# Third block's rounded parts kept in tiles that live on, and the first retention heads' rows loaded and padded one stage earlier

## The reference

```python
x = x + softmax_attention(layernorm(x))     # rope, RMS norm of q and k, 16 heads of 8, causal
x = x + spline_ffn(layernorm(x))
x = x + retention(layernorm(x))             # below
x = x + spline_ffn(layernorm(x))
x = x + linear_attention(layernorm(x))
x = x + conv_moe(layernorm(x))              # MoE block 1: causal attention with rope, then experts
x = x + rwkv(layernorm(x))
x = x + conv_moe(layernorm(x))              # MoE block 2, the same weights

def retention(x):
    q, k = split(x @ W_qk + b_qk); v = x @ W_v + b_v          # 16 heads, q and k 8 wide, v 16 wide
    scores = einsum('bhtd,bhsd->bhts', q, k) * mask            # decay by gamma per head, causal
    denom = clip(abs(scores).sum(-1, keepdims=True), 1.0, 50000.0)
    ret = einsum('bhts,bhsv->bthv', scores / denom, v)
    ret = ret * rsqrt(mean(ret * ret, -1) + EPS)
    return ((x @ W_g + b_g) * ret) @ W_o + b_o
```

## Time and profile before

| | |
|---|---|
| runs, us | 2375.11, 2379.26, 2385.63 |
| profiled execution, its own time | 2386.77 us |
| its span in the trace | 2385.0 us (so 1.77 us lie outside the span) |
| TensorE, mean granted clock | 0.877 of full speed |
| TensorE busy | 1936.0 us, 81% |
| VectorE, ScalarE, GpSimd busy | 1677.1 (70%), 1374.0 (58%), 455.2 us (19%) |
| attention stages begin at | 66.95, 1114.80 and 1803.78 us |
| chunk stage of the retention, then its heads stage | 619.8 to 644.4 us, from 644.6 us |

### The profile page before, as it was taken

The page is one execution under the profiler, slowest core; times in us unless marked ns, Lnnn a source line. Parts: engine busy times, 40 slices in busy tenths (PEclk is TensorE's granted clock), DMA queues, the critical chain, the costliest instruction groups (busy, mean ns, idle before and its releaser), DMA issues. The chain is left out here.

```text
span 2385.0 us, 38939 instructions
## 1 busy us (share of the span) xinstructions
PE 1936.0 (81%) x12970; PEld 1046.3 (44%) x12970; DVE 1677.1 (70%) x4201; ACT 1374.0 (58%) x2027; POOL 455.2 (19%) x816
## 2 busy tenths in 40 slices
PE   5899899975699974687899899957557999999839
PEld 3433333333477753464333333337334333333338
DVE  6688798747466777567798898632696897888423
ACT  4257667865378865435367677832543466677712
POOL 4010120110245430220101110133000010211233
PEclk8599999996899986897699999978865799999959
DMA  7342020001201000006032020014024402200034
GB/s 218 81 72 37 3 38 2 2 33 32 79 38 40 38 18 1 1 1 174 17 59 38 3 38 2 2 47 176 25 59 118 72 13 26 38 2 2 2 106 159
DMA packets 47527, 113.89 MB, mean 48 GB/s; under 512 B 11952, under 2 KB 21426, under 8 KB 43144
## 3 DMA queue, kind: packets, MB, share of 16 engines
q1 hardware_dynamic: 40308, 96.84, 17.2%
q0 software_dynamic: 5088, 11.24, 1.5%
q10 hardware_dynamic: 1964, 3.70, 0.4%
HBM read 62.39 MB, written 32.64 MB: 40 GB/s over the span
## 5 line engine op out<-in xcount | busy, mean ns | idle before, releaser
L1124 ACT ACTIVATE probs<-score 128x1024 f32<-128x1024 f32 x960 | 822.8, 897 | 429.1 <-PE score L1223 423.1
L1294 DVE TENSOR_REDUCE max_part<-stat 128x1 f32<-128x512 f32 x1152 | 724.7, 682 | 94.0 <-PE stat L1175 86.2
L1237 PE MATMUL pv<-probs,v_ones 128*9 128x512 f32 (+3 forms) x3840 | 458.4, 551 | 0.6 <-ACT out_turned L1117 0.6
L1291 DVE CUSTOM_DVE_ANT_0 masked_scores<-stat,mask_row 128x128 f32<-128x128 f32 (+3 forms) x768 | 346.8, 487 | 145.3 <-PE stat L1175 142.2
L1175 PE MATMUL stat<-first_group_k,first_group_q 64*128 64x512 f32 (+2 forms) x960 | 364.2, 496 | 41.5 <-PEq L708 16.1
L1175 PE MATMUL stat<-group_k,group_q 64*128 64x512 f32 (+2 forms) x960 | 337.4, 407 | 16.2 <-DVE max_part L1294 7.7
L1175 PEld LDWEIGHTS stat<-first_group_k,first_group_q 64*128 64x128 f32 x960 | 176.7, 215 | 288.3 <-DVE max_part L1294 174.6
L1175 PEld LDWEIGHTS stat<-group_k,group_q 64*128 64x128 f32 x960 | 157.8, 185 | 279.2 <-DVE max_part L1294 162.1
L1223 PE MATMUL score<-first_group_q,first_group_k 64*128 64x512 f32 x960 | 251.3, 423 | 32.0 <-ACT probs L1124 19.6
L1223 PE MATMUL score<-group_q,group_k 64*128 64x512 f32 x960 | 229.8, 418 | 40.4 <-ACT probs L1124 31.3
L1920 ACT ACTIVATE abs_act_ps<-abs_act_ps 128x1024 f32<-128x1024 f32 (+3 forms) x176 | 167.5, 952 | 46.8 <-PE abs_act_ps L1873 43.2
(11 more groups left out here) (369 smaller groups left out, 2488.7 us busy)
## 6 DMA issues: line engine op xcount, KB each, us to landing
tile_wv<-expert_wv SPq DMA_DIRECT2D x38, 512.0 KB, 3.2
q_parts<-early_parts_t SPq DMA_DIRECT2D x21, 512.0 KB, 3.8
k_parts<-early_parts_t SPq DMA_DIRECT2D x12, 512.0 KB, 4.7
group_k<-k_parts SPq DMA_DIRECT2D x24, 256.0 KB, 11.9
group_q<-q_parts SPq DMA_DIRECT2D x24, 256.0 KB, 18.2
head_q<-q_parts SPq DMA_DIRECT2D x32, 128.0 KB
head_k<-k_parts SPq DMA_DIRECT2D x32, 128.0 KB
first_group_q<-pad_rows SPq DMA_DIRECT2D x6, 512.0 KB, 5.6
```

The lines of the kernel that those rows point to most:

```text
L1124: nc.scalar.activation(probs[:, n % PSLOTS, :, 0:width], sc[m % 2][:, :, 0:width], ACT.Exp, scale=scale).then_inc(slot_read.sem, 1)
L1237: last = nc.tensor.matmul(acc[32 * h:32 * h + D + 1, f:BANK], v9[:, kt, g * HG + h, :], probs[:, (2 * t + h // 2) % PSLOTS, h % 2, 0:BANK ...
L1291: nc.vector.tensor_tensor_reduce(masked[:, at % 2, 0:width], ring[n % RBANKS][:, 0:width], w["mask_row"][:, BANK - width:BANK], 1.0, NEG, ...
L1294: nc.vector.reduce_max(into, ring[n % RBANKS][:], AX.X).then_inc(stat_used.sem, 1)
```

## The change

Three edits go together.

1. The parts of block 2 (the third) are no longer written to `early_parts_t` but to a tile that lives on: `group_q` of the attention, which is now allocated ahead of the qkv stage, or in the retention one slot of `head_q`. Then SyncE's wait for the stores of block 2 is taken out of the qkv stage; the next stage waits for it, where it waited for all stores already.
2. In the retention SyncE loads the rows of heads 0 and 1 in `chunk_stage`, behind its wait for the stores, and GpSimd clears the unused partitions there too, at the end of its own work: four memsets of 4096 columns, for queries and keys. VectorE clears none any more.
3. SyncE's loop over the other 14 heads is written out.

```diff
@@ qkv_stage
-        early = k.sb("early_parts_t", [P, NQ - 1, 2, PARTS, BANK], F32, ctx)
-        parts = [early[:, c] for c in range(NQ - 1)] + [turned_sb]
+        late = len(turned_sb)
+        early = k.sb("early_parts_t", [P, NQ - late, 2, PARTS, BANK], F32, ctx)
+        parts = [early[:, c] for c in range(NQ - late)] + turned_sb
...
-                for c in range(NQ - 1):
+                for c in range(NQ - late):
                     sp.wait_ge(stored[c].sem, stored[c].at(NS))
@@ attention_stage
-        uq, uk = ([first_rows[n], k.sb(f"group_{what}", [P, PAIRS, T], F32, ctx)] for n, what in enumerate("qk"))
+        uq, uk = [first_rows[0], first_rows[2]], [first_rows[1], k.sb("group_k", [P, PAIRS, T], F32, ctx)]
@@ chunk_stage, SyncE
                     wait_parts(sp, parts_stored(k))
+                    for h in range(2):
+                        ahead.load(sp, h, h)
@@ chunk_stage, GpSimd, behind its loop
+                if ahead:
+                    wait_parts(pool, parts_stored(k))
+                    pool.wait_ge(staged.sem, staged.at(NS * NT))
+                    ahead.pad(pool)
@@ new
+class RetentionRows:
+    def load(self, sp, h, par):
+        for a in range(PARTS):
+            at = slice(a * PARTS * D, (a + 1) * PARTS * D)
+            sp.dma_start(self.q[at, par, :], bcast(self.q_dram[h, a], 0, PARTS)).then_inc(self.loaded[par].sem, 16)
+            sp.dma_start(self.k[at, par, :], self.k_dram[h]).then_inc(self.loaded[par].sem, 16)
+    def pad(self, pool):
+        n = 0
+        for tile in (self.q, self.k):
+            for unused in (slice(KROWS, 2 * KROWS), slice(2 * KROWS, P)):
+                n += 1
+                self.nc.gpsimd.memset(tile[unused].rearrange("r b t -> r (b t)"), 0.0).then_inc(self.padded.sem, 1)
+                pool.wait_ge(self.padded.sem, self.padded.at(n))
@@ retention_heads_stage
-                wait_parts(sp, stored)
-                body(0, 0, first=True)
-                body(1, 1, first=True)
-                with sp.Fori(1, H // 2) as n:
-                    for par in range(2):
-                        body(2 * n + par, par)
+                for h in range(2, H):
+                    body(h, h % 2)
...
-                for par in range(2):
-                    for n, rows in enumerate(PADDED):
-                        nc.gpsimd.memset(km[rows, par, :], 0.0).then_inc(k_padded.sem, 1)
-                        pool.wait_ge(k_padded.sem, k_padded.at(2 * par + n + 1))
...
-                for par in range(2):
-                    for rows in PADDED:
-                        nc.vector.memset(qm[rows, par, :], 0.0).then_inc(q_padded.sem, 1)
@@ turned_parts
+    last = k.sb("parts_t", [P, 2, PARTS, BANK], F32, ctx)
+    if spare is None:
+        return [last[:]]
+    return [spare[:, 0].rearrange("p (n a t) -> p n a t", n=2, a=PARTS), last[:]]
```

More of the change, by code:

```diff
@@ L1472, in spline_ffn_stage, with chunk_stage @@
         stats.done()
-def chunk_stage(k, w, kk, v, q_t, k_t, width, keep, out, inner=True):
+def chunk_stage(k, w, kk, v, q_t, k_t, width, keep, out, inner=True, ahead=None):
     nc = k.nc
@@ L1724, in done, with __init__, retention_heads_stage @@
         self.scaled.done(NQ)
-def retention_heads_stage(k, w, v, parts_dram, part, diag, ret, gate, x):
+class RetentionRows:
+    COUNT = 2 * PARTS * 16
+    def __init__(self, k, parts_dram, ctx):
+        self.nc = k.nc
+        self.q, self.k = (k.sb(f"head_{n}", [P, 2, T], F32, ctx) for n in "qk")
+        self.loaded = [k.counter(f"ret_rows_loaded{n}") for n in range(2)]
+        self.padded = k.counter("ret_rows_padded")
+        self.q_dram = parts_dram[0][:, :, 0, :].rearrange("a (h d) t -> h a d t", d=D)
+        self.k_dram = parts_dram[1].rearrange("(h d) a t -> h a d t", d=D)
+    def load(self, sp, h, par):
[10 more added lines that the diff above has]
+                pool.wait_ge(self.padded.sem, self.padded.at(n))
+    def done(self):
+        for sig in self.loaded:
+            sig.done(self.COUNT * H // 2)
+        self.padded.done(4)
+def retention_heads_stage(k, w, v, rows, part, diag, ret, gate, x):
     nc = k.nc
@@ L1758, in retention_heads_stage @@
         o_ps = k.ps("own_out_ps", [P, BANK], ctx)
-        loaded = [k.counter(f"ret_rows_loaded{n}") for n in range(2)]
         a_full, a_used, d_full, d_used = (k.counter("abs_" + n) for n in ("act_full", "act_used", "dve_full", "dve_used"))
@@ L1965, in _ @@
                 take_out(H - 1)
-        for par in range(2):
-            loaded[par].done(NL * H // 2)
+        rows.done()
         cleared.done(5)
-        q_padded.done(4)
-        k_padded.done(4)
         a_full.done(NA * H)
@@ L2465, in first_group_rows, with turned_parts @@
 def first_group_rows(k, ctx):
[L2466 to L2471 removed]
+    return [k.sb(f"{name}", [P, PAIRS, T], F32, ctx) for name in ("first_group_q", "first_group_k", "group_q")]
+def turned_parts(k, ctx, spare=None):
+    last = k.sb("parts_t", [P, 2, PARTS, BANK], F32, ctx)
+    if spare is None:
+        return [last[:]]
+    return [spare[:, 0].rearrange("p (n a t) -> p n a t", n=2, a=PARTS), last[:]]
 def softmax_layer(k, w, qkv, wo, parts_dram, rows, parts_t, x, turns=(), first_norm=None):
     y = qkv[:, :, 0:C]
[L2477 removed]
+    attention_stage(k, w, qkv, parts_dram, rows, parts_t[-1], float(D) ** -0.5, y, first_norm)
     output_stage(k, w, [(y, wo)], x, turns)
@@ L2504, in retention_layer @@
                 transpose_stage(k, [(qkv[:, :, 0:C], q_t)], w["ident"])
-                chunk_stage(k, w, qkv[:, :, C:2 * C], qkv[:, :, 2 * C:], q_t, None, VD, w["bd16"][:], ret, inner=False)
-        retention_heads_stage(k, w, qkv[:, :, 2 * C:], parts_dram, part, diag, ret, gate, x)
+                chunk_stage(k, w, qkv[:, :, C:2 * C], qkv[:, :, 2 * C:], q_t, None, VD, w["bd16"][:], ret, inner=False, ahead=rows)
+        retention_heads_stage(k, w, qkv[:, :, 2 * C:], rows, part, diag, ret, gate, x)
         output_stage(k, w, [(gate[:, :, b * C:(b + 1) * C], w["w_o_r"][:, b, :]) for b in range(2)], x,
```

37 lines of the change are left out of this document (12 added, 25 removed).

## The result

The changed kernel took 2374.94 us (median of 19 runs, 2365.51 to 2383.22), the kernel before 2380.80 us beside it (19 runs, 2375.11 to 2391.14). The ratio is 0.9965, 95% interval 0.9953 to 0.9977: faster by 8.3 us, or 5.5 to 11.2 (the ratio is that of the means, 2373.77 and 2382.06 us; the medians lie 5.9 us apart). Forecast were -9.9 us and 2369.4 us. The sign and the main places were right; two terms of the sum were too small, with opposite signs, so that the total came out nearer than its parts.

A forecast was written before the change was run, and what follows sets the result against it. No engine bounds the whole, so stage seams were read. Terms -4.6 - 4.5 + 0.6 - 0.2 - 1.2 gave -9.9 us, 2369.4 us (chance 0.62); terms' range -7.5 to -11.8, 8-in-10 range 2361 to 2379 us.

The forecast's parts named there:

- The waits that go: End of the qkv stage in MoE blocks 1 and 2: SyncE's store wait disappears, -4.6 and -4.5 us.
- What is late next: Start of both MoE attentions: block 1's row loads contend with stores still running, 0 to 0.8 us a block, +0.6 together.
- Shifted by 4.6 us, the last load is issued at 1115.3 and lands at 1117.2: MoE block 1's attention start: row loads keep their issue pace and landing delay, only 4.6 us earlier.
- rival C: MoE attention starts: SyncE held up issuing, loads as late as before; about -2 us left, 2377 us; chance 0.10.
- Retention, end of its qkv stage: SyncE's store wait there ends barely later than ScalarE's store: -0.2 us, bounds 0 and -0.6.
- Heads: Retention's chunk-to-heads seam: DMA wait gone, GpSimd's clears end the chunk stage; -1.2 us, range -0.4 to -2.1.
- it waits for TensorE each time: Retention heads: SyncE's written-out loop changes nothing, 0 us.
- First block: End of its qkv stage: VectorE's last cast hides SyncE's wait, so 0 us.
- its terms' own range: Whole sum with contention, heads and retention terms at their ends: -7.5 to -11.8 us.
- rival D: Retention's chunk stage: GpSimd's memsets at twice the price, ending at 669, about +3 us; chance 0.02.
- A: MoE attentions: TensorE's clock stays up after the shorter gap; -18 us in all, 2361 us; chance 0.15.
- B: MoE attentions: clock falls into block 2's pattern, 8.2 us each; with two blocks 2385.8 us; chance 0.11.

The follow-up runs named there:

- e4: Changed kernel with the third block's three stores issued in the softmax layers' attention, behind the loads of block 1's rows; 2371.96 us, ratio 0.9946.
- e13: Changed kernel with clears behind the norm, third block's stores behind block 1's loads, ScalarE's last-block stores behind its copy of v; 2359.01 us, ratio 0.9893.
- e1: Kernel before with the first edit and the written-out loop; retention heads' rows loaded and cleared in the heads stage as before; 2376.48 us, ratio 0.9974.
- e2: Changed kernel with SyncE's wait for the third block's stores put back, so only the early rows and clears and the written-out loop; 2383.44 us, ratio 1.0003.
- e11: Changed kernel with three quarters of GpSimd's clears moved into the retention's qkv stage, behind VectorE's first-block decay; 2364.51 us, ratio 0.9905.
- e3: Changed kernel with ScalarE's two stores of the last block started behind its copy of v; one execution, 2374.34 us.

## Why the prediction was right, point by point

*The waits that go* (-4.6 and -4.5): the attention begins 4.5 and 4.4 us earlier, counted from VectorE's last cast. From SyncE's last store to the attention's start it was 0.65 us, not 0.5. Right.

*What is late next* (+0.6 for both, bounds 0 to 1.6): 1.24 and 0.87 us are lost by the copy-out, 2.1 together, and 1.03 and 1.01 by the turn. This is one of the two mis-sized terms, and it lies outside its bounds. The step that failed is "Shifted by 4.6 us, the last load is issued at 1115.3 and lands at 1117.2". The load was not issued as before and then late by its bytes; the issue itself slowed, so that the last load is issued 7.05 us behind the attention's beginning instead of 5.09. e4 shows that the third block's stores in front, SyncE's own, are the cause: with them out of the way it is 5.0 again (3.6 and 4.4 in e13, where ScalarE's stores are out of the way too). It is the mechanism of rival C at a quarter of its price. The other part of the step, that 0.8 us of delay are free because the turn waits for GpSimd anyway, was right in kind and put a little low: rows 2.0 us late, turn 1.0 us late in both blocks, so 1.0 us was free. The first copy-out is late by what the turn is, within the 0.6 us by which two traces of the same code differ there.

*Retention, end of its qkv stage* (-0.2): 0.03 us, from the spline addition to the chunk stage. ScalarE's store was the last already.

*Heads* (-1.2): from the chunk stage's last copy to TensorE's first matmul 12.78 us before, 11.19 after: -1.6. The memsets took 14.2 us as worked out; they ended at 652.5 instead of 655.0 because the whole stage lies 2.5 us earlier, most of it from the first block; and TensorE began 0.5 us behind them. One reading of the rows was incomplete, without harm: only 3.5 of the 5.1 us lay behind all memsets before, since VectorE's last one ended at 653.6.

Behind TensorE's first matmul another 1.9 us came. This is the other mis-sized term: the sum ends at that matmul and puts what comes after it at nothing, so that the heads gained 3.4 us in all (2.3 without head 14, below), outside the bounds of 0.4 to 2.1. The first head takes 0.5 us less: the granted clock, 0.50 at first in both, rises to 1.00 some 7 us into it instead of 9 (over the first 10 us 0.63 instead of 0.53). At head 3 (counted from 0) TensorE waited 0.37 us for its rows before and 0.16 after, which gives 0.2 us; the other traces have from 0.1 to 0.5 there. And 1.05 us lie at head 14, where it waited before and not after:

```profile
847.81 0.66 PE L1883 MATMUL abs_dve_ps<-head_q,head_k 128*128 128x128 f32 x4 [0.90 <-DMA head_k<-k_parts]
```

That is the place of the third edit, which the prediction put at 0, "it waits for TensorE each time". It does, but with the written-out loop the last of the four loads was issued 2.7 us into nearly every head instead of 3.2 to 3.3, and in both traces the DMA engines still moved these rows until about 1 us before the next head. None of the twelve traces with the written-out loop has this wait, e1 included; the one with the loop has it at one head of fourteen. Whether it is the edit or chance, no run here separates.

*First block* (0): from its attention's beginning to the first copy-out 45.1 us instead of 45.5, but 45.6 in e1, which has the same edit there, and 44.9 in e2, which hasn't; from there to the last copy-out 403.7 instead of 403.8. Nothing that can be told from chance.

*Sum by the traces*: -4.5 + 1.2 - 4.4 + 0.9 - 1.6 - 0.5 - 0.2 - 1.1 = -10.2 us, against -8.3 by the ratio (5.5 to 11.2) and -9.9 forecast. That the total is so near is partly luck: the heads gained 3.4 us instead of 1.2, which more than made up for the contention that was put 1.5 us too low. Two sums of the prediction are off without bearing on this: the upper end of its terms' own range is -7.9 (-9.1 + 1.6 - 0.4), not -7.5, and rival D would leave about +4 us, not +3.

*Rivals.* A and B did not happen: clocks 0.54 and 0.74 in block 1 as before, and in block 2 the second stretch's pattern at 0.70 again. C happened in part. D did not: the memset price from the rows' slope held to 0.1 us. Where the clock did give something was at the start of the heads (0.5 us), where no rival looked for it. The changed kernel's median lay 5.5 us above the predicted one: 1.5 us of that is the kernel before, which measured 2380.80 us beside it instead of 2379.26, and the rest is the smaller difference.

*The point missed in the plan of the change*: GpSimd's clears were read rightly as the new end of the chunk stage, 10.6 us behind ScalarE, and not followed to what that is worth. e11 shows 13.6 us there, more than the whole change.

## What to carry to other kernels

A wait that is taken out of a stage's end leaves its transfers running into the next stage, in front of whatever the same queue issues there: look what that queue is asked for first, and let the next stage's urgent loads be issued before the stores that nobody waits for. Work moved to an idle engine should go to that engine's idle time, not to its end; and where it is a clear on GpSimd, beside VectorE's two-input operations and not beside its TENSOR_SCALARs. When a seam is timed, count from a computing instruction in front of it to one behind it, since whole executions differ by more than the seam.

## What the runs showed of the hardware

- At the start of the MoE attentions SyncE issued four key loads in 4.66 to 4.80 us with some 1.5 MB of its own stores just started (3.43 and 3.46 in e3, without ScalarE's stores beside them), and in 2.26 to 2.40 us without (1.70 and 2.14 in e13, without ScalarE's either).
- Behind an idle TensorE (11.6 us in the changed kernel) the heads' first 10 us ran at a granted clock of 0.63, behind 1.1 us of idling in e11 at 1.00; the first head took 3.05 us less.
- A clear on GpSimd held a TENSOR_SCALAR of VectorE for its whole length (3.49 us instead of 0.17), while RECIPROCAL and TENSOR_TENSOR kept theirs.
- Loads with a leading dimension of 2 ran at 0.12 of the DMA engines, 51 GB/s, and doubled the landing time of a fill queued behind them (30.5 us instead of 15.0).
- The same attention, from first to last copy-out, took one of a few lengths: 402.3 to 405.3 us in 21 of 39 cases (13 traces, three attentions each), the others between 407.6 and 412.1, in any of the three blocks and in kernels that don't differ there. The tail behind the last took about 121.3 or 123.5 us. The lengths go with the granted clock: 0.98 or 0.99 over each of the 21 short ones, 0.95 to 0.97 over each of the 18 long ones. Whole executions of one kernel go with it as well: of 19 runs of the changed kernel the fastest had a mean clock of 0.887 (2365.51 us) and the slowest 0.873 (2383.22 us). What decides the clock in an execution was not found.
